# Routes of a two-layer transformer block: target row and weight in the table of routes, with one VectorE instruction per column

## The reference

```
topk_w, topk_idx = jax.lax.top_k(probs, K)                 # K = 2
topk_w = topk_w / jnp.sum(topk_w, axis=-1, keepdims=True)
gate_full = zeros((T, E)).at[arange(T)[:, None], topk_idx].add(topk_w)
for e in range(E):
    h = silu(xf @ w1[e].T) * (xf @ w3[e].T)
    out = out + gate_full[:, e:e + 1] * (h @ w2[e].T)
```

## Time and profile before

| | |
|---|---|
| median of 3 runs | 2340.03 us (2338.78 to 2341.39) |
| the profiled execution | 2340.75 us |
| its span in the profile | 2339.0 us |
| mean granted TensorE clock | 0.943 of full speed |
| PE busy | 2034.9 us (87%) |
| DVE busy | 1365.6 us (58%) |
| ACT busy | 1513.5 us (65%) |
| loop of the first route | DVE's line 932 first starts at 229.39 us |
| loop of the second route | first at 1820.35 us, last at 1844.27 us |

### The profile page before, as it was taken

How to read it: one execution, slowest core, us unless ns; L and a number is a source line. 1 busy time by engine, 2 the same in 40 slices (tenths; PEclk the granted TensorE clock), 3 DMA queues, 4 the chain that set the end, 5 groups by cost and what they waited for, 6 DMA issues and landing times. The chain is left out here.

```text
span 2339.0 us, 43032 instructions
## 1 busy us (share of the span) xinstructions
PE 2034.9 (87%) x13329; PEld 970.5 (41%) x13330; DVE 1365.6 (58%) x3004; ACT 1513.5 (65%) x2495; POOL 463.8 (20%) x395
## 2 busy tenths in 40 slices
PE   5997799960996999999999999999863699999994
PEld 3786555540662222222222222222252467667663
DVE  5567544438787444444445555554147787777773
ACT  2215333324674999999999999999963344444442
POOL 0030277752000000000000000000000143344341
PEclk9998899985997999999999999999986799999997
DMA  5006377763100000000002222222174477767774
GB/s 200 1 1 225 82 154 152 151 149 154 43 29 1 1 2 1 1 2 1 1 19 73 73 73 73 73 73 73 55 243 148 173 178 174 173 174 174 172 173 129
DMA packets 157317, 225.11 MB, mean 96 GB/s; under 512 B 14080, under 2 KB 130992, under 8 KB 157184
## 3 DMA queue, kind: packets, MB, share of 16 engines
q1 hardware_dynamic: 129376, 184.04, 25.3%
q0 software_dynamic: 27264, 37.24, 9.4%
q10 hardware_dynamic: 544, 2.10, 0.3%
HBM read 157.63 MB, written 65.57 MB: 95 GB/s over the span
## 5 line engine op out<-in xcount | busy, mean ns | idle before, releaser
L1800 ACT ACTIVATE at_pexp<-at_psS 128x1024 f32<-128x1024 f32 x1024 | 942.7, 1163 | 30.7 <-PE at_psS L1707 30.7
L1816 DVE TENSOR_REDUCE at_mx<-at_psM 128x1 f32<-128x512 f32 x474 | 327.3, 691 | 413.8 <-PE at_psM L1735 410.2
L1722 PE MATMUL at_psO<-at_pexp,at_vst 128*32 128x512 f32 x4096 | 546.0, 605 | 3.5 <-ACT at_pexp L1800 0.8
L1707 PE MATMUL at_psS<-l1c_QT,l1c_KT 64*128 64x512 f16 x2048 | 412.7, 385 | 16.2 <-ACT at_pexp L1800 9.8
L1707 PEld LDWEIGHTS at_psS<-l1c_QT,l1c_KT 64*128 64x128 f16 x2048 | 105.4, 93 | 536.5 <-ACT at_pexp L1800 498.6
L2149 PE MATMUL ex_psH<-wide_wgu,ex_xT 128*128 x1278 | 259.9, 357 | 0.6 <-issue 0.6
L986 POOL DMA_INDIRECT sums<-ex_y,top_dst x107 | 170.0, 1589 | 280.1 <-ACT ex_y L2205 226.6
L2220 DVE SCALAR_TENSOR_TENSOR ex_bias<-ex_psH,top_w_scale,ex_bias 128x456 f32<-128x456 f32 x213 | 147.4, 692 | 76.6 <-PE ex_psH L2149 60.3
L2193 ACT ACTIVATE ex_sg<-ex_bias 128x228 f32<-128x228 f32 x213 | 83.7, 393 | 152.3 <-DVE ex_bias L2220 152.3
L972 POOL DMA_INDIRECT ex_xg<-normed,top_tok x142 | 140.1, 987 | 197.6 <-POOLq L81 148.7
L1735 PE MATMUL at_psM<-at_ksumT,l1c_QT 64*128 64x512 bf16 x474 | 178.8, 377 | 0.0
(11 more groups left out here) (359 smaller groups left out, 2735.8 us busy)
## 6 DMA issues: line engine op xcount, KB each, us to landing
ex_bias<-in_L_ffn_bg SPq DMA_DIRECT2D x71, 342.0 KB, 4.7
ex_bias<-in_L_ffn_b SPq DMA_DIRECT2D x71, 342.0 KB, 5.5
ex_piece<-in_L_ffn_W SPq DMA_DIRECT2D x48, 228.0 KB, 2.7
l1c_KT<-in_L_ffn_W SPq DMA_DIRECT2D x32, 342.0 KB, 3.4
halves<-l1c_KT SPq DMA_DIRECT2D x32, 342.0 KB, 3.2
wide_wgu<-halves SPq DMA_DIRECT2D x8, 1368.0 KB
ex_b<-in_L_ffn_b SPq DMA_DIRECT2D x71, 128.0 KB
normed<-rt_area SPq DMA_DIRECT2D x16, 512.0 KB, 2.6
```

Of the source, the lines that this page charges most:

```text
L1707: mm = pe.matmul(psS[:, unit[use], hh * BANK:(hh + 1) * BANK], keys(k.KT, p)[r, kt * P:(kt + 1) * P], keys(k.QT, p)[r, c * BANK:(c + 1) * ...
L1722: mm = pe.matmul(psO[g * VW:(g + 1) * VW, :], vst[:, p % 2, hh, kt, :], pexp[:, (p * ST + step) % 3 * 2 + n, hh * BANK:(hh + 1) * BANK], s ...
L1800: act.activation(pexp[:, u % 6, :], psS[:, unit["score", u // (ST * 2), u % (ST * 2)], :], ACT.Exp, scale=D ** -0.5 / (QS * QS)).then_inc( ...
L1816: dve.tensor_reduce(mx[:, n:n + 1], psM[:, :], AX.X, ALU.max).then_inc(reduced, 1)
```

## The change

The buffer `hiEq` goes. The comparison with `hi` and the product with the row number are one instruction (`scalar_tensor_tensor`: compare with a per-partition scalar, then multiply by a tensor), and since that scalar, `hi[:, t, j:j+1]`, is one value in each partition, an instruction does one column of 71, and a group takes four. ScalarE now reads `oneHi[.., 0, :]`, which holds the row number and not 1, and so its scale is the weight over the row number: two instructions (a reciprocal of `row` and a product into `w12`) replace the two copies into `dstv`. `matched` is raised by the fourth of the narrow instructions, `hot` by the comparison with `lo`.

```diff
-        hiEq = area[:, at:at + 2 * PG * NTILE].rearrange("p (r n c) -> p r n c", r=2, n=PG)
-        at += 2 * PG * NTILE
...
-                        ins = act.activation(oneHi[:, n % 2, m, 1, :], hiEq[:, n % 2, m, :], ACT.Copy,
+                        ins = act.activation(oneHi[:, n % 2, m, 1, :], oneHi[:, n % 2, m, 0, :], ACT.Copy,
                                              scale=w12[:, t, j:j + 1])
...
                 ser(dve.tensor_scalar(row[:, :], k.lane[:, 0:NT], k.lane_row[:, 0:1], 1.0, ALU.add, ALU.add))
-                ser(dve.tensor_copy(dstv[:, :, 0], row[:, :]))
-                ser(dve.tensor_copy(dstv[:, :, 1], row[:, :]))
+                ser(dve.reciprocal(row2[:, :], row[:, :]))
+                ser(dve.tensor_tensor(w12[:, :, :], w12[:, :, :], row2[:, :].unsqueeze(2).to_broadcast([P, NT, 2]), ALU.mult))
...
-                    dve.tensor_tensor(hiEq[:, r, :, :], lanes(NTILE), wide(hi, n, NTILE),
-                                      ALU.is_equal).then_inc(matched, 1)
-                    dve.tensor_tensor(oneLo[:, r, :, :], lanes(P), wide(lo, n, P), ALU.is_equal)
-                    dve.wait_ge(matched, n + 1)
-                    dve.tensor_tensor(oneHi[:, r, :, 0, :], hiEq[:, r, :, :], wide(dstv, n, NTILE),
-                                      ALU.mult).then_inc(hot, 1)
+                    for m in range(PG):
+                        t, j = (n * PG + m) // 2, m % 2
+                        ins = dve.scalar_tensor_tensor(oneHi[:, r, m, 0, :], k.lane[:, 0:NTILE], hi[:, t, j:j + 1],
+                                                       row[:, t:t + 1].to_broadcast([P, NTILE]), ALU.is_equal, ALU.mult)
+                    ins.then_inc(matched, 1)
+                    dve.tensor_tensor(oneLo[:, r, :, :], lanes(P), wide(lo, n, P), ALU.is_equal).then_inc(hot, 1)
```

## The result

Slower. The changed kernel has a median of 2349.23 us over 12 runs (2342.79 to 2356.93), the kernel before 2340.41 over 12 (2337.28 to 2342.70); the ratio is 1.0038, 95% interval 1.0027 to 1.0049, which is 8.9 us (6.3 to 11.5). The forecast was 2347.3 with a range of 2343.0 to 2350.5. A second set of five runs gave 1.0037 (1.0023 to 1.0052). The profiled execution took 2342.81, at the low end of its kernel; its span is 2341.1 us.

A forecast was written before the change was run, and what follows sets the result against it. The round trip line 932, ScalarE, TensorE, buffer free was taken as the loop's bound; the terms sum to 3.46 us a route, 6.9 for two, giving 2347.3 us, range 2343.0 to 2350.5.

The forecast's parts named there:

- step 2: First two pairs of groups in the loop: 0.45 us more, then 0.33 where TensorE's slow clock absorbs the rest.
- step 3: Five full pairs from the fifth group to the fifteenth, 0.45 us more each: 2.25 us a route.
- step 4: Fifteenth to sixteenth group: VectorE's own pace decides, 1.43 us instead of 1.34, so 0.09 more.
- step 6: End of the loop, last group's line 932 to line 945: 3.47 us instead of 3.35, so 0.12 more.
- step 7: Ahead of the loop: reciprocal and product take 0.65 us where the two copies took 0.43, so 0.22 more.
- rival A: Narrow pass in the loop is cheap, 0.15 us start to start: 3.1 us in all, 2343.1 to 2343.9; chance 0.13.
- B: In the loop TensorE waits for VectorE's third result, so cheap passes shorten the round trip: 2339.1 us; chance 0.05.
- C: Narrow passes in the loop don't overlap, four take 1.16 us: 11.9 us more in all, 2352.3; chance 0.06.
- D: TensorE, less busy in the loop, might stay at its lower clock: 15.4 us more in all, 2355.8; chance 0.04.

The follow-up runs named there:

- padded kernels: Kernel before with each route's last small VectorE instruction repeated: both routes 11.2 and 9.1 us slower, first route only 3.0, second only 0.0 and 3.7.

## Why the prediction was right

Step by step for the second route, profile against profile, in us more than before:

| step | predicted | profiles |
|---|---|---|
| first pair (step 2) | 0.45 | 0.45 (4.44 against 3.99) |
| second pair, slow clock (step 2) | 0.33 | 0.05 (3.82 against 3.77) |
| five steady pairs (step 3) | 2.25 | 2.24 (17.07 against 14.83) |
| fifteenth to sixteenth (step 4) | 0.09 | 0.16 |
| the end (step 6) | 0.12 | 0.14 |
| ahead of the loop (step 7) | 0.22 | 0.22 |
| sum | 3.46 | 3.26 |

The price of the pass, which no row had in this form, was 0.29 and 0.205 and came out at 0.287 and 0.203. The rows of line 2237, with 384 columns, and the pace of line 1281 gave it; the two kernels with doubled passes show that the pointer scalar is what separates this price from rival A's.

One term was mis-sized: the second pair. It took the third group to run at the lower clock from end to end. In this execution the clock rose while that group ran, and gave back 0.28.

Step 4 has a false mechanism, at little cost. It let VectorE's own pace, 1.43 us, decide from the fifteenth group to the sixteenth. In this route the buffer decides: the matmuls of 1844.58 end at 1845.79, and VectorE starts at 1845.82, 1.49 us after 1844.33. In the first route of the same profile the distance is 1.68, with VectorE waiting for TensorE:

```profile
256.69 0.91 DVE L932 SCALAR_TENSOR_TENSOR rt_area<-top_lane,rt_hi,rt_row 128x71 f32<-128x71 f32 x4 [0.17 <-PE rt_psL L806]
```

The second profile has 1.66 and 1.42. A pair takes 3.42 in all four routes; how it divides between the two buffers differs, and only the most uneven division is VectorE's pace.

In the first route the count is different in each execution: 30.9 and 31.0 against 28.1 and 27.3, so 2.8 to 3.7. The routes of all the profiles with the old loop, the padded kernels included, have a mean of 27.4 and 27.9, those of the changed one 30.95 and 31.25: 6.9 in sum, the predicted 6.9. The agreement to a tenth is luck in part: in the second route steps 2 and 4 miss on opposite sides, and the first route comes out between 2.8 and 3.7 with the profiles taken. The timed 8.9 has 6.9 in its interval, and the 2 us between them are not explained. The stated range alone doesn't separate the forecast from A, whose 2343.1 lies in it too; the pair of 3.42 us does.

The prediction named as a sign of being wrong that something after the gather moves by more than the routes do. In the first pair of profiles the first layer's experts moved by 3.2 us, as much as a route; the second profile of the kernel before moves there by 3.4 with no change, so this was scatter.

The claim that the round trip through ScalarE is the bound was tested from both sides: making ScalarE's leg short (one signal for each pass) took the whole loss away, and a third buffer, which hides the leg in either kernel, made both faster than they were with two.

- A, the cheap pass: false by 58 ns a pass.
- B, TensorE waiting for VectorE's last result: false in both kernels, as `hot` is raised 0.3 and 0.67 us too early to matter; TensorE does wait for that result once ScalarE starts per pass (243.69), with passes that are not cheap and VectorE's pace as the bound.
- C, no overlap: false. The Trainium skill's "VectorE: DVE Perf Modes", section "The DRAIN you can't avoid", has the next operation wait for an empty pipe; the passes start 84 ns before the one ahead is done (287 less 203), also where a pointer scalar is read. The measurement decides, and its allowance for operations that nothing holds fits.
- D, the clock: false here; 1.00 from the fourth group on in both routes. A fall inside the loop was seen only in the kernel with doubled passes. Its price was not added up in full: with 1.1 us in five pairs the terms named there give 6.7 us a route, not 7.7.

## What to carry to other kernels

In a loop that goes round between engines through a pair of buffers, and in which no engine is full, an instruction's price is what it puts in front of the first signal that another engine waits for, not what it adds to its engine's busy time: here VectorE's own pace rose by 0.08 us a group (1.34 to 1.42), and the loop by 0.22. When a wide instruction is split by columns, the signal should be split with it, or the split charges the whole sum to the one who waits. And where the round trip is the bound, a third buffer can hide it: it was worth 5.8 us of 2341 here. What a cheaper instruction would be worth in this loop was not run.

## What the runs showed of the hardware

- A pointer scalar on VectorE costs 60 ns in an instruction's duration (286 against 226) and 58 ns in the pace of back-to-back ones (203 against 145), 71 float32 columns. I had expected 54.
- In the kernel with doubled passes, after a stretch in which TensorE was busy for 2.95 of 6 us, the granted clock fell (0.72 as the mean of the next 6 us) while the loop went on, and VectorE waited 0.71 us for a buffer.
- The same kernel can start behind a pause of TensorE at the lower clock or at the full one: 17 against 29 matmul records in the same eight us of the first layer's experts, granted 0.57 against 1.00, and 3.4 us between the two executions in that stage. Two sets of 11 and 12 runs of one program, on two chips, differ by 3.7 us, over half of the 6.9 that the change adds in the routes; whether the clock is behind that too was not measured.
